# Deformable sampling: half of the odd samples' corner sums go from Pool to ACT and DVE

## Chip, core and metric

The kernel runs on one core of a Trainium2 chip. The metric is the device time of one execution in microseconds (us). PE is TensorE (matrix products and transposes into PSUM), DVE is VectorE, ACT is ScalarE, Pool is GpSimd, SP issues the DMAs.

## What is computed

The program is a network of four blocks on an input of 8 x 64 x 16 x 16; the change lies in the second block's convolution, a deformable one. Each output pixel samples its input at 9 positions that an earlier convolution has shifted, for each of 4 groups of 16 channels; a sample is the sum of 4 neighbouring pixels, each by a bilinear weight. The samples are contracted with the weights `wd`.

```python
def deform_conv(x, offset, wd, k=3, pad=1, dg=4):
    ...
    py = dy + ky[None, None, :, None, None] + hh[None, None, None, :, None]
    px = dx + kx[None, None, :, None, None] + ww[None, None, None, None, :]
    y0 = jnp.floor(py)
    x0 = jnp.floor(px)
    ...
    val = gather(y0, x0) * (wy0 * wx0)[:, :, None] + gather(y0, x0 + 1) * (wy0 * wx1)[:, :, None] + gather(y0 + 1, x0) * (wy1 * wx0)[:, :, None] + gather(y0 + 1, x0 + 1) * (wy1 * wx1)[:, :, None]
    wr = wd.reshape(wd.shape[0], dg, cg, K)
    return jnp.einsum('ogck,bgckhw->bohw', wr, val)
```

## The kernel before

Each stage of the network is a block with one hand-written instruction queue for each engine; semaphores order the engines among each other. The stage in question works on 36 samples (4 channel groups x 9 positions). The 2048 output pixels are 16 tiles of 128 partitions. For sample s:

- SP loads the sample's pixel numbers, spread over all partitions, into one of four buffers BC (512 KB a load), as soon as the masks of sample s-4 are made.
- DVE makes a 0/1 mask of the lower half of the pixels from BC (`compare`, L1279), ACT the mask of the upper half (L1202). Three buffers hold masks, so the masks of sample s wait for the gather of s-3.
- PE gathers (`gather`, L1096): 64 products of mask and pixel values into two PSUM banks, 4 to 7 in turn. It gives the 4 corners by 16 channels for each tile. It waits for both masks of s and for the weighing of s-2.
- DVE weighs the corners (`weigh`, L1289): two products of 128x512 that read PSUM and write U, of which there are two (SQ and SD). Weighing s waits for Pool's sums of s-2.
- Pool adds the four corners: a first sum of 128x512 into V1 (L1032), a wait for that, and a second of 128x256 into VAL (L1035). The last sample's sums are made by DVE (L1302, L1303).

DVE's queue in the loop is: compare(s+1), weigh(s). After eight samples PE turns their values (`contract`, L1117): 16 transposes in four groups of four. Each group fills a PSUM bank, 0 and 1 in turn, and ACT empties it into VTA (`evac`, L1195). Then PE projects them (`project`, L1130). In PE's queue the turnings stand after the gathers of samples 11, 19, 27 and 34, the projections after those of 15, 23 and 31 and at the end; a fifth turning and projection, of samples 32 to 35, follow. ACT empties the first three turnings after its masks of samples 13, 21 and 29. "First turning" and so on are these calls of `contract`; a group of eight samples is the time from one turning to the next.

Of the kernel before, what the change touches and what calls it, by code (L numbers as in the profile page):

```python
# [74 lines left out]
def build(nc, x_dram, packs, idx_dram, gate_dram, out_dram):  # L75
    with ExitStack() as ctx:
# [19 lines left out]
        def wt(name, a=0, n=None, p0=0, p1=P):  # L96
# [6 lines left out]
        w_in = [w_sems[0 if n == 0 else 2 - n % 2] for n in range(len(SECTIONS))]  # L103
        W_AT = [16 if n == 0 else 16 * ((n + 1) // 2) for n in range(len(SECTIONS))]
        stored = sem("stored")
        ln_centered, ln_squared, ln_var, ln_sd, ln_rstd, ln_spread, ln_placed, ln_copied, ln_done = (sem(n) for n in (
            "ln_centered", "ln_squared", "ln_var", "ln_sd", "ln_rstd", "ln_spread", "ln_placed", "ln_copied", "ln_done"))
        g_ps, g_exp, g_sum = (sem(n) for n in ("g_ps", "g_exp", "g_sum"))
        x_half = sem("x_half")
        EARLY = range(1, 7)  # L110
# [99 lines left out]
        def ln_dve(dve, n, out_of):  # L210
            o, view = out_of(0)
            dve.wait_ge(ln_squared, 2 * n + 1)
            dve.tensor_copy(o, view(bank(0))).then_inc(ln_placed, 1)
            for h in range(2):
                c = slice(h * STAT, (h + 1) * STAT)
                dve.wait_ge(ln_sd, 2 * n + h + 1)
                dve.reciprocal(SD[:, c], SD[:, c]).then_inc(ln_rstd, 1)
            for h in range(2):
                o, view = out_of(h)
                if h:  # L220
                    dve.wait_ge(ln_copied, n + 1)
                else:
                    dve.wait_ge(ln_placed, n + 1)
                dve.wait_ge(ln_spread, 2 * n + h + 1)
                spread = PS[:, 2048 * (1 - h):2048 * (2 - h)].rearrange("p (q c) -> p q c", q=4)[:, :, 0:P]
                if view is flat_view:
                    quarters = o.rearrange("p (q c) -> p q c", q=4)
                    ins = dve.tensor_tensor(quarters, quarters, spread, ALU.mult)  # L228
                else:
                    for b in range(2):  # L230
                        part = o[:, b].rearrange("p (k r) w -> p k r w", k=2)
                        ins = dve.tensor_tensor(part, part, spread[:, 2 * b:2 * b + 2].rearrange("p k (r w) -> p k r w", w=W), ALU.mult)
                ins.then_inc(ln_done, 1)
# [720 lines left out]
        with ExitStack() as sctx, nc.Block() as block:  # L954
# [35 lines left out]
                sem("s3_" + n) for n in ("y_pad", "c1_ps", "h_act", "h_dve", "tents_ready", "c2_ps", "gx_ps", "gx_hi", "gx_done", "idx_ready",  # L990
                "frac_ready", "idxt_ps", "idxt_in", "idx_out", "oh_ready", "ga_ps", "u_ready",
                "val_ready", "vt_ps", "vt_in", "dc_ps", "xs_ready"))
            vt_dve, wc_ready, last_val = sem("s3_vt_dve"), sem("s3_wc_ready"), sem("s3_last_val")

            bc_in = [sem(f"bc_in{i}") for i in range(NBC)]

# [27 lines left out]
            @block.gpsimd  # L1024
            def _(pool):
                pool.memset(YP[:, :, :], 0.0).then_inc(y_pad, 1)  # L1026
                for k in range(3):
                    pool.memset(HS3[k][:, :, :], 0.0).then_inc(y_pad, 1)
                for s in range(SAMPLES - 1):

                    pool.wait_ge(u_ready, s + 1)
                    after_pool(pool, pool.tensor_tensor(V1[:, :, :, :], U[s % 2][:, :, 0:2, :], U[s % 2][:, :, 2:4, :], ALU.add))  # L1032
                    if s >= 16 and s % 8 == 0:
                        pool.wait_ge(vt_ps, 4 * (s // 8 - 1))
                    pool.tensor_tensor(VAL[:, (s // 8) % 2, :, s % 8, :], V1[:, :, 0, :], V1[:, :, 1, :], ALU.add).then_inc(val_ready, 1)  # L1035
                    pool.wait_ge(val_ready, s + 1)

            @block.tensor
            def _(pe):
# [60 lines left out]
                def contract(ch):  # L1100

                    ns = min(8, SAMPLES - 8 * ch)
                    rows = ns * CG
                    pe.wait_ge(val_ready, min(8 * ch + ns, SAMPLES - 1))
                    if ch == 4:
                        pe.wait_ge(last_val, 1)
                    for j, q in enumerate(LAST if ch == 4 else range(4)):
                        n = 4 * ch + j
                        if n == 19:
                            pe.wait_ge(vt_dve, 1)  # L1110
                        elif n >= 2:
                            pe.wait_ge(vt_in, n - 1)
                        for i in range(4):

                            t = 4 * (2 * (q % 2) + i // 2) + 2 * (q // 2) + i % 2
                            src = VAL[:, ch % 2, t, 0:ns, :].rearrange("p s c -> p (s c)")
                            mm = pe.transpose(bank(j % 2)[0:rows, i * P:(i + 1) * P], src, wt("ident"))  # L1117
                        mm.then_inc(vt_ps, 1)
                    return rows

# [28 lines left out]
            @block.scalar  # L1149
            def _(act):  # L1150
                act.wait_ge(y_pad, 1)
                ln_act(act, 2, "epsc", padded_y)
                act.wait_ge(w_in[3], W_AT[3])
                act.wait_ge(y_pad, 4)
                act.wait_ge(c1_ps, 1)
                for k in range(3):

                    a, b = max(0, 1 - k), min(W, W + 1 - k)
                    act.activation(pair(HS3[k], 0, 2, 0)[:, :, :, a:b], images(bank(6))[:, :, :, a + k - 1:b + k - 1],
                                   ACT.Identity, bias=wt("c1b")).then_inc(h_act, 1)  # L1160

                def corners(n):
                    bl, qh = n // 2, n % 2
                    act.wait_ge(gx_ps, n + 1)
                    act.activation(GX[:, 0, qh, bl, :, :], bank(n % 4).rearrange("p (k c) -> p k c", k=4), ACT.Copy,
                                   scale=GSCALE).then_inc(gx_hi, 1)

                def tents(n):
                    act.wait_ge(frac_ready, n + 1)
                    for u, at in ((U0, 0.0), (U1, -1.0)):  # L1170
                        o = tiles4(u[:, :, :], n)
                        after_act(act, act.activation(o, tiles4(PY[:, :, :], n), ACT.Abs, bias=at if at == 0.0 else wt("minus1")))
                        act.activation(o, o, ACT.Relu, bias=1.0, scale=-1.0).then_inc(tents_ready, 1)

                for n in range(4):
                    corners(n)
                for n in range(3):
                    tents(n)
                for n in range(NB):
                    act.wait_ge(idxt_ps, n + 1)  # L1180
                    act.activation(tiles_of(IDXT[:, :], n), bank(4 + n).bitcast(FP16)[0:SAMPLES, 0:HC].rearrange("q (h c) -> q h c", h=2),
                                   ACT.Copy).then_inc(idxt_in, 1)
                for n in range(4, 2 * NB):
                    corners(n)

                tents(3)
                warm(act, ACT.Abs_reciprocal_sqrt)

                def evac(ch):
                    rows = P if ch < 4 else 64  # L1190
                    for j, q in enumerate(LAST if ch == 4 else range(4)):
                        if ch == 4 and j % 2:
                            continue
                        act.wait_ge(vt_ps, 4 * ch + j + 1)
                        act.activation(VTA[0:rows, ch % 4, q * 512:(q + 1) * 512], bank(j % 2)[0:rows, :], ACT.Copy,  # L1195
                                       scale=16.0 / GSCALE).then_inc(vt_in, 1)
                for s in range(SAMPLES):

                    act.wait_ge(bc_in[s % NBC], 16 * (s // NBC + 1))
                    if s >= NOH:  # L1200
                        act.wait_ge(ga_ps, s - NOH + 1)
                    act.activation(OHU[:, s % NOH, :], BC[:, s % NBC, :], ACT.Abs_reciprocal_sqrt, bias=wt("hitq"),  # L1202
                                   scale=HIT, saturate=False).then_inc(upper_ready, 1)
                    if s >= 13 and s % 8 == 5:
                        evac(s // 8 - 1)
                evac(3)
                evac(4)

                warm(act, ACT.Sqrt)

            @block.vector
            def _(dve):
# [68 lines left out]
                def weigh(s):  # L1281
# [7 lines left out]
                        ins = dve.tensor_tensor(o, src, w, ALU.mult)  # L1289
                    ins.then_inc(u_ready, 1)  # L1290

                compare(0)
                compare(1)
                dve.wait_ge(wc_ready, NB)
                for s in range(SAMPLES):
                    if 1 <= s < SAMPLES - 1:
                        compare(s + 1)
                    weigh(s)
                last = SAMPLES - 1
                sums = PY[:, :, :].rearrange("p t k -> p (t k)")[:, 0:TILES * 2 * CG].rearrange("p (t k c) -> p t k c", k=2, c=CG)  # L1300
                dve.wait_ge(u_ready, last + 1)
                after(dve, dve.tensor_tensor(sums, U[last % 2][:, :, 0:2, :], U[last % 2][:, :, 2:4, :], ALU.add))  # L1302
                dve.tensor_tensor(VAL[:, (last // 8) % 2, :, last % 8, :], sums[:, :, 0, :], sums[:, :, 1, :], ALU.add).then_inc(last_val, 1)  # L1303
                for j in (1, 3):
                    q = LAST[j]
                    dve.wait_ge(vt_ps, 16 + j + 1)
# [1101 lines left out]
```

## Time and profile before

| what | us |
|---|---|
| three runs | 539.71, 541.76, 542.22 (median 541.76) |
| the profiled execution | 541.19 |
| its span, first to last instruction | 539.4 |
| sample loop, first gather to fifth turning | 218.2 to 315.6 |
| busy in the span: PE, DVE, ACT, Pool | 478.7, 328.7, 293.0, 140.1 |

The span's whole chain passes through many stages; the change touches one. So what counts is who waits for whom between 218 and 316 us, and which engine has no idle time there. In the rows below a timeline's columns are start, duration, engine, line, operation, output and inputs, count of instructions merged in the row, and in brackets the idle time of the engine just before with what ended it. Instructions of PE follow each other in a pipeline, so a row's end lies a little after the next row's start.

### The profile page before, as it was taken

To read this page: it belongs to the slowest core of one execution; us is meant where nothing else is said; L and a number is where in the kernel's file an instruction comes from. 1 tells how busy PE (TensorE), PEld (TensorE's weight loads), DVE (VectorE), ACT (ScalarE), POOL (GpSimd) and SP (SyncE) were. 2 spreads that over 40 slices of the span, in tenths; PEclk is the share of its full clock that TensorE was granted. 3 is DMA by queue.
4 is the path that set the end of the run, shared out by engine and by line. 5 is a ranking of instruction groups with operands and counts; after the bars stand their busy time and mean duration, and the time that the engine had idled before them with its cause. 6 is when DMAs were issued, how large, how long until landed. Compare 5 with 4: busy or idle time off the path is not lost. (4 is left out here: it accounts for less than half of the span.)

```text
span 539.4 us, 12786 instructions
## 1 busy us (share of the span) xinstructions
PE 478.7 (89%) x5459; PEld 255.5 (47%) x5464; DVE 328.7 (61%) x575; ACT 293.0 (54%) x430; POOL 140.1 (26%) x134
## 2 busy tenths in 40 slices
PE   4799998998996999878998999997997998999992
PEld 1343432554333496778788744343223335533330
DVE  1285999455356366677777746758554593554565
ACT  2583223526651236988788636674683171665561
POOL 8170000000064000599999920003402000000000
PEclk9999999998998899999999998999899889999998
DMA  7000000002661002855565200011003000001000
GB/s 271 2 2 2 1 2 1 1 12 104 162 155 34 2 1 63 293 206 194 202 201 196 81 6 18 0 67 48 0 1 125 0 2 1 2 21 40 1 18 22
DMA packets 9801, 34.52 MB, mean 64 GB/s; under 512 B 1248, under 2 KB 2704, under 8 KB 9360
## 3 DMA queue, kind: packets, MB, share of 16 engines
q1 hardware_dynamic: 9744, 33.70, 19.5%
q8 instruction: 43, 0.70, 0.5%
q14 instruction: 14, 0.11, 0.1%
HBM read 32.94 MB, written 0.75 MB: 62 GB/s over the span
## 5 line engine op out<-in xcount | busy, mean ns | idle before, releaser
L1096 PE MATMUL PS<-GX,OH 128*128 128x64 f16 x1152 | 70.4, 193 | 10.0 <-DVE OH L1279 7.1
L1202 ACT ACTIVATE OHU<-BC,wbuf 128x2048 fp8e4<-128x2048 f16 x36 | 70.0, 1994 | 12.5 <-PE PS L1096 8.8
L1096 PEld LDWEIGHTS PS<-GX,OH 128*128 128x128 f16 x1152 | 67.6, 98 | 15.1 <-DVE OH L1279 8.9
L1096 PE MATMUL PS<-GX,OHU 128*128 128x64 f16 x1152 | 70.1, 193 | 0.1
L1096 PEld LDWEIGHTS PS<-GX,OHU 128*128 128x128 fp8e4 x1152 | 67.6, 98 | 0.1
L1035 POOL TENSOR_TENSOR VAL<-V 128x256 f32<-128x256 f32 x35 | 38.8, 1108 | 2.7
L708 DVE SCALAR_TENSOR_TENSOR D<-QKVP,wbuf,D 128x1024 f32<-128x1024 f32 x27 | 34.6, 1281 | 7.7 <-ACT D L608 6.9
L1032 POOL TENSOR_TENSOR V<-SQ 128x512 f32<-128x512 f32 x18 | 25.1, 1394 | 49.9 <-DVE SQ L1289 48.6
L437 PE MATMUL PS<-T,DG 128*32 128x512 f32 x336 | 37.1, 594 | 0.0
L1996 PE MATMUL PS<-Y,wbuf 64*128 64x512 f32 x128 | 35.6, 618 | 0.1
L2069 ACT ACTIVATE HID<-PS,wbuf 128x512 f32<-128x512 f32 x44 | 28.7, 689 | 10.4 <-PE PS L1996 10.3
L164 PE MATMUL PS<-X,wconst 128*128 128x512 f32 x32 | 19.6, 709 | 15.1 <-DMA wconst<-pack_dram 7.7
L1289 DVE TENSOR_TENSOR SQ<-PS,WC 128x512 f32<-128x512 f32 x36 | 23.2, 686 | 14.8 <-PE PS L1096 8.5
L824 POOL TENSOR_TENSOR ACC<-T 128x512 f32<-128x512 f32 x2 | 2.5, 1270 | 107.3 <-DVE T L938 107.3
L1279 DVE TENSOR_SCALAR OH<-BC,wbuf 128x2048 f16<-128x2048 f16 x36 | 28.1, 780 | 3.7 <-DMA BC<-idx_dram 3.7
L203 ACT ACTIVATE SQ<-PS 128x512 f32<-128x512 f32 x16 | 9.4, 595 | 38.3 <-POOL VTA L1026 11.8
L2008 PE MATMUL PS<-HID,wbuf 128*64 128x512 f32 x128 | 29.9, 601 | 0.0
L1289 DVE TENSOR_TENSOR SD<-PS,WC 128x512 f32<-128x512 f32 x36 | 23.1, 684 | 10.6 <-POOL VAL L1035 7.6
L1996 PEld LDWEIGHTS PS<-Y,wbuf 64*128 64x128 f32 x128 | 14.5, 185 | 20.3 <-issue 9.4
L608 ACT ACTIVATE D<-PS,wbuf 128x512 f32<-128x512 f32 x12 | 8.3, 689 | 28.6 <-PE PS L437 28.6
L893 ACT ACTIVATE HID<-PS,wbuf 128x512 f32<-128x512 f32 x32 | 19.4, 692 | 8.1 <-PE PS L834 8.1
L1032 POOL TENSOR_TENSOR V<-SD 128x512 f32<-128x512 f32 x17 | 22.0, 1295 | 1.3
(296 smaller groups left out, 920.3 us busy)
## 6 DMA issues: line engine op xcount, KB each, us to landing
BC<-idx_dram SPq DMA_DIRECT2D x36, 512.0 KB, 4.3
GB<-gate_dram SPq DMA_DIRECT2D x16, 256.0 KB, 7.2
wbuf<-pack_dram SPq DMA_DIRECT2D x1, 1913.0 KB, 9.3
wbuf<-pack_dram SPq DMA_DIRECT2D x1, 1624.0 KB, 6.7
wbuf<-pack_dram SPq DMA_DIRECT2D x1, 1494.0 KB, 6.1
wbuf<-pack_dram SPq DMA_DIRECT2D x1, 871.0 KB, 4.3
wbuf<-pack_dram SPq DMA_DIRECT2D x1, 788.0 KB, 10.8
wbuf<-pack_dram SPq DMA_DIRECT2D x1, 607.0 KB, 3.8
```

Of the source, the lines that this page charges most:

```text
L164: pe.matmul(bank(h), wt("center"), X[:, h * HC:(h + 1) * HC], start=True, stop=True).then_inc(ln_centered, 1)
L437: mm = pe.matmul(bank(DBANK[t % 2] + n)[32 * q:32 * q + 32, :], DG[:, (2 * j + hf) * NBLK + i, :], src, start=(i == blocks[0]), stop=(i == ...
L708: ins = dve.scalar_tensor_tensor(out=d, in0=window(QKVP[j], dy, dx), scalar=wt("dw5", j * 25 + 5 * dy + dx, 1), in1=d, op0=ALU.mult, op1=A ...
L1032: after_pool(pool, pool.tensor_tensor(V1[:, :, :, :], U[s % 2][:, :, 0:2, :], U[s % 2][:, :, 2:4, :], ALU.add))
L1035: pool.tensor_tensor(VAL[:, (s // 8) % 2, :, s % 8, :], V1[:, :, 0, :], V1[:, :, 1, :], ALU.add).then_inc(val_ready, 1)
L1096: mm = pe.matmul(o, (OH, OHU)[qh][:, s % NOH, t * P:(t + 1) * P], src, start=(qh == 0 and part == 0), stop=(qh == 1 and part == 1))
L1202: act.activation(OHU[:, s % NOH, :], BC[:, s % NBC, :], ACT.Abs_reciprocal_sqrt, bias=wt("hitq"), scale=HIT, saturate=False).then_inc(uppe ...
L1279: dve.tensor_scalar(OH[:, s % NOH, :], BC[:, s % NBC, :], wt("qidx"), 0.0625, ALU.is_equal, ALU.mult).then_inc(oh_ready, 1)
L1289: ins = dve.tensor_tensor(o, src, w, ALU.mult)
L1996: pe.matmul(bank(UBANK[(n + bh) % 4]), wt("w1_3", e * FH3 + m * P, P, r, r + C), Y[r:r + C, bp * HC:(bp + 1) * HC], start=True, stop=True, ...
L2008: pe.matmul(bank(OBANK[j % 3])[C * bh:C * bh + C, :], wt("w2_3", (2 * e + m) * C, C), HID[:, (n + i) % HBUF, :], start=(m == 0), stop=(m = ...
L2069: act.activation(HID[:, n % HBUF, :], bank(UBANK[n % 4]), ACT.Relu, bias=wt("b1_3", 2 * e + m, 1)).then_inc(hid_in_a, 1)
```

## The change

For odd samples below 32 Pool makes the first sum only, into VO (two buffers, one for each second odd sample). ACT copies one of its two halves into PSUM bank 1 (VP), after its mask of sample s+4. DVE adds the other half and VP into VAL (`corner_sum`), in its queue after the compare of s+4 and ahead of the weighing of s+3. Since bank 1 is taken, the first three turnings use bank 0 alone: each group of four transposes waits until ACT has emptied the one before. In the fourth turning the second group waits for the first's evacuation, and the two banks are used in turn. The layer norm gives up a semaphore of its own (`ln_placed`) and waits on DVE's step counter.

```diff
+            def sums_on_dve(s):
+                return s % 2 == 1 and s < 32
+            def turned(j, ch):
+                return bank(j % 2 if ch >= 3 else 0)
...
                     pool.wait_ge(u_ready, s + 1)
+                    if sums_on_dve(s):
+                        if s >= 5:
+                            pool.wait_ge(val_dve, s // 2 - 1)
+                        pool.tensor_tensor(VO[:, (s // 2) % 2, :, :, :], U[s % 2][:, :, 0:2, :], U[s % 2][:, :, 2:4, :], ALU.add).then_inc(val_ready, 1)
+                        continue
...
                     if ch == 4:
-                        pe.wait_ge(last_val, 1)
+                        pe.wait_ge(val_dve, 17)
+                    else:
+                        pe.wait_ge(val_dve, 4 * ch + 4)
...
-                        elif n >= 2:
+                        elif ch >= 3 and j >= 2 or ch == 4:
                             pe.wait_ge(vt_in, n - 1)
+                        elif n:
+                            pe.wait_ge(vt_in, n)
...
-                            mm = pe.transpose(bank(j % 2)[0:rows, i * P:(i + 1) * P], src, wt("ident"))
+                            mm = pe.transpose(turned(j, ch)[0:rows, i * P:(i + 1) * P], src, wt("ident"))
...
+                    j = s - NOH - 1
+                    if j >= 0 and sums_on_dve(j):
+                        act.wait_ge(val_ready, j + 1)
+                        if j >= 3:
+                            act.wait_ge(val_dve, j // 2)
+                        act.activation(VP, VO[:, (j // 2) % 2, :, 1, :], ACT.Copy).then_inc(vp_in, 1)
...
+                def corner_sum(s):
+                    dve.wait_ge(vp_in, s // 2 + 1)
+                    if s >= 16:
+                        dve.wait_ge(vt_ps, 4 * (s // 8 - 1))
+                    dve.tensor_tensor(VAL[:, (s // 8) % 2, :, s % 8, :], VO[:, (s // 2) % 2, :, 0, :], VP, ALU.add).then_inc(val_dve, 1)
...
                     if 1 <= s < SAMPLES - 1:
                         compare(s + 1)
+                    if s >= 3 and sums_on_dve(s - 3):
+                        corner_sum(s - 3)
                     weigh(s)
```

## Rows read from the trace of the kernel before

**Rows 1.** Busy time by stretch: stretch, length, each engine's busy time, PE clock, DMA.

```profile
236.00:246.00 10.00, 7.58 (x242) 7.11 (x239) 7.22 (x12) 7.43 (x5) 9.37 (x9) 1.00 0.58 207
```

**Rows 2.** The weighings' line (L1289), what ended DVE's idle time: us, times.

```profile
  POOL VAL L1035: 13.9, 20
```

**Rows 3.** Timeline of Pool in the loop.

```profile
237.86 1.27 POOL L1032 TENSOR_TENSOR V<-SQ 128x512 f32<-128x512 f32 x1
239.22 1.21 POOL L1035 TENSOR_TENSOR VAL<-V 128x256 f32<-128x256 f32 x1
240.51 1.28 POOL L1032 TENSOR_TENSOR V<-SD 128x512 f32<-128x512 f32 x1
```

**Rows 4.** Timeline of DVE: a weighing in the same cycle.

```profile
240.53 1.29 DVE L1289 TENSOR_TENSOR SQ<-PS,WC 128x512 f32<-128x512 f32 x2 [0.69 <-POOL VAL L1035]
```

**Rows 5.** Timeline of PE: gather 11, the first turning, gather 12.

```profile
245.18 0.23 PE L1096 MATMUL PS<-GX,OH 128*128 128x64 f16 x2 [0.60 <-DVE OH L1279]
...
247.06 1.07 PE L1117 MATMUL PS<-wconst,VAL 128*128 128x128 f32 x8
...
248.38 1.15 PE L1117 MATMUL PS<-wconst,VAL 128*128 128x128 f32 x8 [0.25 <-ACT VTA L1195]
...
249.36 0.22 PE L1096 MATMUL PS<-GX,OH 128*128 128x64 f16 x2
```

**Rows 6.** Timeline of PE: gather 14, the first projection, gather 16.

```profile
253.78 0.23 PE L1096 MATMUL PS<-GX,OH 128*128 128x64 f16 x2 [0.52 <-DVE OH L1279]
...
257.62 1.94 PE L1130 MATMUL PS<-VTA,wbuf 128*64 128x512 f32 x8
...
259.49 0.20 PE L1096 MATMUL PS<-GX,OH 128*128 128x64 f16 x1
```

**Rows 7.** Timeline of PE: starts of turnings two and three, and gather 35.

```profile
268.30 0.31 PE L1117 MATMUL PS<-wconst,VAL 128*128 128x128 f32 x1
...
289.92 0.31 PE L1117 MATMUL PS<-wconst,VAL 128*128 128x128 f32 x1
...
310.94 0.22 PE L1096 MATMUL PS<-GX,OH 128*128 128x64 f16 x2
```

**Rows 8.** Timeline of Pool: sums ahead of a compare, behind one, and alone.

```profile
252.44 0.73 POOL L1035 TENSOR_TENSOR VAL<-V 128x256 f32<-128x256 f32 x1
...
295.73 1.65 POOL L1032 TENSOR_TENSOR V<-SQ 128x512 f32<-128x512 f32 x1 [0.61 <-DVE SQ L1289]
297.45 1.25 POOL L1035 TENSOR_TENSOR VAL<-V 128x256 f32<-128x256 f32 x1
...
311.41 1.28 POOL L1032 TENSOR_TENSOR V<-SQ 128x512 f32<-128x512 f32 x1
```

**Rows 9.** Timeline of DVE at the same places as rows 8.

```profile
251.43 1.29 DVE L1289 TENSOR_TENSOR SQ<-PS,WC 128x512 f32<-128x512 f32 x2 [1.01 <-PE PS L1096]
252.64 1.08 DVE L1279 TENSOR_SCALAR OH<-BC,wbuf 128x2048 f16<-128x2048 f16 x1
...
295.50 0.74 DVE L1279 TENSOR_SCALAR OH<-BC,wbuf 128x2048 f16<-128x2048 f16 x1
296.16 1.29 DVE L1289 TENSOR_TENSOR SD<-PS,WC 128x512 f32<-128x512 f32 x2
297.36 0.75 DVE L1279 TENSOR_SCALAR OH<-BC,wbuf 128x2048 f16<-128x2048 f16 x1
```

**Rows 10.** DVE's second sum of the last sample: ns, least, median, most.

```profile
L1303 DVE TENSOR_TENSOR VAL<-PY x1: 426/426/426, 315.1 to 315.1; 128x256 f32<-128x256 f32 x1
```

**Rows 11.** A short operation of ACT, by groups: busy us, mean ns, idle before.

```profile
L206 ACT ACTIVATE SD<-PS,wconst 128x64 f32<-128x64 f32 x2 | 0.6, 311 | 0.4 <-PE PS L183 0.4
```

**Rows 12.** Timeline of ACT: an evacuation and four masks in a row.

```profile
247.73 0.60 ACT L1195 ACTIVATE VTA<-PS 128x512 f32<-128x512 f32 x1 [1.05 <-PE PS L1117]
...
271.30 7.67 ACT L1202 ACTIVATE OHU<-BC,wbuf 128x2048 fp8e4<-128x2048 f16 x4
```

**Rows 13.** Timeline of PE: inside gather 26.

```profile
287.93 0.20 PE L1096 MATMUL PS<-GX,OH 128*128 128x64 f16 x1 [1.36 <-issue]
```

More of the change, by code:

```diff
@@ L105, in build @@
         stored = sem("stored")
-        ln_centered, ln_squared, ln_var, ln_sd, ln_rstd, ln_spread, ln_placed, ln_copied, ln_done = (sem(n) for n in (
-            "ln_centered", "ln_squared", "ln_var", "ln_sd", "ln_rstd", "ln_spread", "ln_placed", "ln_copied", "ln_done"))
+        ln_centered, ln_squared, ln_var, ln_sd, ln_rstd, ln_spread, ln_copied, ln_done = (sem(n) for n in (
+            "ln_centered", "ln_squared", "ln_var", "ln_sd", "ln_rstd", "ln_spread", "ln_copied", "ln_done"))
         g_ps, g_exp, g_sum = (sem(n) for n in ("g_ps", "g_exp", "g_sum"))
@@ L212, in ln_dve @@
             dve.wait_ge(ln_squared, 2 * n + 1)
-            dve.tensor_copy(o, view(bank(0))).then_inc(ln_placed, 1)
+            steps["dve"] += 1
+            placed = steps["dve"]
+            dve.tensor_copy(o, view(bank(0))).then_inc(dve_step, 1)
             for h in range(2):
@@ L222, in ln_dve @@
                 else:
-                    dve.wait_ge(ln_placed, n + 1)
+                    dve.wait_ge(dve_step, placed)
                 dve.wait_ge(ln_spread, 2 * n + h + 1)
@@ L992, in build @@
                 "val_ready", "vt_ps", "vt_in", "dc_ps", "xs_ready"))
-            vt_dve, wc_ready, last_val = sem("s3_vt_dve"), sem("s3_wc_ready"), sem("s3_last_val")
+            vt_dve, wc_ready, val_dve, vp_in = sem("s3_vt_dve"), sem("s3_wc_ready"), sem("s3_val_dve"), sem("s3_vp_in")
+            VO = sb("VO", [P, 2, TILES, 2, CG], F32, sctx)
+            VP = bank(1, TILES * CG).rearrange("p (t c) -> p t c", c=CG)
+            def sums_on_dve(s):
+                return s % 2 == 1 and s < 32
+            def turned(j, ch):
+                return bank(j % 2 if ch >= 3 else 0)
             bc_in = [sem(f"bc_in{i}") for i in range(NBC)]
@@ L1194, in evac @@
                         act.wait_ge(vt_ps, 4 * ch + j + 1)
-                        act.activation(VTA[0:rows, ch % 4, q * 512:(q + 1) * 512], bank(j % 2)[0:rows, :], ACT.Copy,
+                        act.activation(VTA[0:rows, ch % 4, q * 512:(q + 1) * 512], turned(j, ch)[0:rows, :], ACT.Copy,
                                        scale=16.0 / GSCALE).then_inc(vt_in, 1)
@@ L1302, in _ @@
                 after(dve, dve.tensor_tensor(sums, U[last % 2][:, :, 0:2, :], U[last % 2][:, :, 2:4, :], ALU.add))
-                dve.tensor_tensor(VAL[:, (last // 8) % 2, :, last % 8, :], sums[:, :, 0, :], sums[:, :, 1, :], ALU.add).then_inc(last_val, 1)
+                dve.tensor_tensor(VAL[:, (last // 8) % 2, :, last % 8, :], sums[:, :, 0, :], sums[:, :, 1, :], ALU.add).then_inc(val_dve, 1)
                 for j in (1, 3):
```

## Prediction

> Everything below is worked against the profiled execution of the kernel before: 541.19 us, of which 539.4 are its span and 1.8 lie around it. The median of the runs shown is 541.76, so a difference found here would stand 0.6 higher against that. G(s), W(s), C(s) stand for sample s's gather on PE, weighing on DVE (L1289) and compare on DVE (L1279).
>
> **What bounds the kernel now.** I read the busy time by stretch first, then who waited for whom, then the timelines. In the sample loop Pool is the busiest engine, 9.37 of 10 us, with PE at 7.58 and its clock at 1.00 [rows 1]. Weighing waited 20 times for Pool's second sum [rows 2]. The timelines give the cycle: Pool's first sum starts at 237.86 and again at 240.51, so a sample costs 2.65 us: 1.28 for the first sum, 1.21 for the second, two gaps of 0.08 [rows 3]; the next weighing starts 0.1 after the second sum ends and had waited 0.69 [rows 4]. But a group of eight samples also holds a turning (16 transposes) and a projection, and there PE has hardly any slack. A gather has 1.88 us from its start to the next work (245.18 to 247.06), the first turning 2.30 (to 249.36) [rows 5], a projection 1.87 [rows 6]. 8 x 1.87 + 2.30 + 1.87 = 19.1 us of PE work, and the groups take 268.30 - 247.06 = 21.24 and 289.92 - 268.30 = 21.62 [rows 5, 7]. So Pool's relief can win at most some 2.3 us a group before PE is the bound.
>
> **Pool, odd samples below 32.** The second sum leaves Pool. Its price there is 0.73 when nothing disturbs it [rows 8] and 1.21 here, because DVE's compare and Pool's sums shut each other out: a sum that begins 0.1 behind a compare takes 1.25 in place of 0.73, or 1.65 in place of 1.28; a compare that begins 0.2 behind a sum took 1.08 and ended 0.55 after it [rows 8, 9]. For two samples Pool then holds two first sums (2 x 1.28), one second (0.73), three gaps (0.25) and still two compares that push in (0.5 each): 4.5 us, 2.25 a sample in place of 2.65. Pool stays the bound until the first turning: DVE needs 2 x (1.21 + 0.66) + 0.35 = 4.1 a pair (1.21 and 0.66 are the distances between the starts of its operations, 0.35 that of the corner sum, each 0.08 less than it lasts), and G(s+2) follows G(s) by at least 2.07 to W, 1.21 to C, 0.74 for C and 0.06 to PE = 4.08 [rows 5, 6, 9]. Samples 4 to 11 run so; the first of them is still paced by loads and PE, so I take 7.3 of them x 0.40 = **2.9 us gained by the first turning** (bounds: 2.0 and 4.3, by 4.75 and by 4.1 us a pair).
>
> **The two new operations.** DVE adds 16 corner sums of 128x256. The same shape took 0.43 [rows 10]; that its second operand lies in PSUM I cost at nothing, since two 128x512 weighings, which read PSUM too, take 1.29, and Pool's first sum beside them keeps its 1.28 [rows 3, 4, 8]. 16 x 0.43 = 6.9 us, all beside PE and Pool except one (below). The sum stands before W(s), so weighing and every compare behind it queue on ACT's copy. For odd j that copy stands behind ACT's mask of j+4, which starts when G(j+1) ends; the corner sum stands behind C(j+4), which follows W(j+2), and so comes about 1 us after the copy. ACT adds 16 copies of 128x256 to PSUM, which no row shows: between 0.31 (128x64) and 0.60 (128x512), by proportion 0.43 [rows 11, 12]. A pair on ACT is 2 x 1.9 + 0.4 = 4.2, under 4.5. Behind them wait ACT's masks and its evacuations. In a group ACT is just in time: from the end of G(16) it has three masks and two copies, 3 x 1.9 + 2 x 0.35 = 6.4, and the next turning's first values are ready after 6.4. With copies of 0.60 it is 0.5 late, twice.
>
> **One bank for the turned values.** This is the costly part. Before, PE turned two groups of four back to back and waited only 0.25 for the third [rows 5]. Now, in the first three turnings, each group waits until ACT has emptied the bank: first transpose to evacuation 0.67 (247.06 to 247.73), evacuation 0.60, back to PE 0.06: 1.32 a round [rows 5, 12]. Three rounds and the last group's issue, 3 x 1.33 + 0.49 = **4.5 in place of 2.3: 2.2 us each**. In the fourth, only its second group waits for the first's evacuation and the last for the second's: 2 x 1.32 + 0.49 = 3.1, 0.8 more.
>
> **The groups after.** PE: 4.5 + 8 x 1.87 + 1.87 + two waits of 0.34 (the 4.08 above against 2 x 1.87, once behind the turning, once behind the projection; between them DVE catches up) = **22.0 us**. Pool's 4 x 4.5 = 18.0 no longer matters: the bound has moved to PE. Against 21.24 and 21.62 that is +0.75 and +0.4. The last stretch, from the third turning to G(35) (310.94 - 289.92 = 21.0 before [rows 7]), has seven gathers: 4.5 + 7 x 1.87 + 1.87 + 0.7 = 20.1, then the fourth turning waits 0.35 for the last corner sum, which DVE reaches only behind C(35) (a compare delayed, or not, sets this: 0 to 0.8), and takes 3.1: 23.6, +2.6. After G(35) nothing is changed.
>
> **A stall that was covered.** In the second of these groups PE stood 1.36 us inside a gather, put down to issue [rows 13]. Pool was the bound there, so part of it was covered: that group took 21.62 against 21.24. In the new kernel PE is the bound and the same stall counts whole, on top of the 22.0. It may not come back (0) or come as it was (1.36); the instructions around it are the same, so I take the row, 1.36. The Trainium skill's page "Runtime: NRT & Kernel Launch", section "Instruction fetch mechanics", says that fetching code across a block boundary is mostly hidden; if this is such a fetch and hidden the next time, the sum below is smaller by 1.36. The row shows only that it was not hidden here.
>
> Costed at nothing: the layer norm's own semaphore given up for DVE's step counter (the same wait on the same copy); PE's extra wait on the corner sums before the first three turnings (the sum of the group's last odd sample is done 1.5 us earlier, by the order on DVE); Pool's wait for a free half of VO (two odd samples back). No DMA is added; the loads of BC are asked for by the same masks.
>
> **Sum:** 541.19 - 2.9 + 0.75 + 0.4 + 2.6 = 542.0, and with the stall 543.4; from the unrounded terms **543.3 us**.
>
> **The rivals.**
> (a) The stall does not return: **542.0**. For it: one gather of 36 shows it. Against: the same code at the same place.
> (b) Slower, the compare loses to Pool's second sum. In an even-odd pair C(s+3) is ready 0.08 before Pool could start the second sum of s. The trace shows it winning by 0.09 (297.36 against 297.45) and the sum then taking 1.25 [rows 8, 9]. If it comes 0.1 later it waits out 0.73 and ends 0.62 later: G(15) and G(19) of every group are late by that, 2 x 0.62 x 3 = 3.7, and the first stretch gains 2.0 only: 543.3 + 3.7 + 0.9 = **547.9**. It decides from a shift of 0.1 us, such as a longer corner sum makes. The Trainium skill's page "SBUF — State Buffer", section "Who interferes with whom", has it as an exclusive lock that whoever issues first holds for a whole instruction; the rows above agree (0.55 after the sum's end). Whoever drops this sentence keeps the rows.
> (c) ACT is late: copies at 0.60 bring 2 x 0.5, and evacuations a little: **544.5**.
> (d) Faster, the rounds of the one bank stay off the path: a group would be 19.1 + 0.7 = 19.8, and the stage would win 2.9 + 1.4 + 1.8 + 0.9 = 7: **534**. Against: the waits are in PE's own queue ahead of the next gather, and PE has 2.1 us to spare a group where they cost 2.2. For: should weighing and compares now run far enough ahead, some of PE's other waits go too.
> (e) The copy is not what delays, but the change does not relieve Pool (a compare hits all three sums): 5 us a pair, and the first stretch gains 1: **545**.
>
> **How the numbers follow.** Forecast with stall 0.36, (a) 0.24, (b) 0.13, (c) 0.10, (d) 0.10, (e) 0.07. The range runs from 540.0 ((a) with the first stretch at its better bound) to 547.0 (the unknown copy and most of (b)). About 0.5%, 2.7 us, is what a measurement of this kernel can tell from no change. From 541.19 that puts (a) and seven tenths of the forecast's own scatter inside, with a fifth of (c); (b), (e), the rest of (c) and of the forecast above, less what the better bound of the first stretch takes back; (d) below: same 0.52, slower 0.37, faster 0.11.
>
> **What would show it.** First turning at 244 us in place of 247; distances between turnings of 22 to 23.4; three PE waits for ACT of some 0.8 in each of the first three turnings; Pool idle between an odd sample's sum and the next; PE waiting for DVE's masks by 0.3 and not 0.6. It is wrong if turnings stay near 2.3, if the groups fall under 21 us, or if compares of 1.1 and more become common.

## The result: 0.85% slower, and the profile after

Twenty runs of the changed kernel have a median of 545.38 us (540.51 to 552.67), twenty of the kernel before 539.65 (535.89 to 542.83). The ratio is 1.0085, with a 95% interval of 1.0054 to 1.0115, or some 4.6 us; it leaves out runs over 1.5% above the kernel's fastest, six of the changed kernel's twenty, so it is below the 5.7 us between the medians. The profiled execution took 544.75 us, its span 542.9. Forecast were 543.3 (540.0 to 547.0): the time lies in the range, but the loss is a bit more than twice the 2.1 us forecast, and the outcome that was given most weight, no change within 0.5%, is not the one that came.

Stretch by stretch the costs that the forecast names came close to their sizes. Pool's timeline in the first stretch, two samples:

```profile
236.48 1.71 POOL L1049 TENSOR_TENSOR V<-SQ 128x512 f32<-128x512 f32 x1
238.27 1.25 POOL L1052 TENSOR_TENSOR VAL<-V 128x256 f32<-128x256 f32 x1
239.59 1.28 POOL L1047 TENSOR_TENSOR VO<-SD 128x512 f32<-128x512 f32 x1
240.99 1.71 POOL L1049 TENSOR_TENSOR V<-SQ 128x512 f32<-128x512 f32 x1
```

The pair lasts 240.99 - 236.48 = 4.51 us, two samples before 5.29 [rows 3]. Both sums of the even sample stand behind a compare here, at 1.71 and 1.25; not all do (see rival (b) below). The two new operations, by line (ns: least, median, most), DVE's corner sum and ACT's copy:

```profile
L1323 DVE TENSOR_TENSOR VAL<-VO,PS x16: 406/411/417, 230.2 to 312.7; 128x256 f32<-128x256 f32 x16
```

```profile
L1230 ACT ACTIVATE PS<-VO x16: 363/367/376, 229.3 to 310.9; 128x256 f32<-128x256 f32 x16
```

Both are a little cheaper than 0.43 [rows 10 to 12]. PE's timeline of the first turning shows the rounds through one bank:

```profile
246.00 0.31 PE L1138 MATMUL PS<-wconst,VAL 128*128 128x128 f32 x1
...
247.32 0.33 PE L1138 MATMUL PS<-wconst,VAL 128*128 128x128 f32 x1 [0.69 <-ACT VTA L1216]
...
248.66 0.33 PE L1138 MATMUL PS<-wconst,VAL 128*128 128x128 f32 x1 [0.69 <-ACT VTA L1216]
...
250.01 0.33 PE L1138 MATMUL PS<-wconst,VAL 128*128 128x128 f32 x1 [0.69 <-ACT VTA L1216]
...
250.50 0.19 PE L1113 MATMUL PS<-GX,OH 128*128 128x64 f16 x1
```

PE waits 0.69 for ACT three times, and 250.50 - 246.00 = 4.50 us pass where 2.30 did [rows 5]. Behind it the bound has changed. What ended DVE's idle time before the weighings (us, times), in the kernel before:

```profile
  PE PS L1096: 11.5, 10
```

and in the kernel after:

```profile
  PE PS L1113: 23.3, 12
  POOL VAL L1052: 2.6, 7
```

Weighing waits for PE where it waited 13.9 us for Pool [rows 2]. Two stretches behind the first turning, with the columns of rows 1 (behind the length come the busy times of PE, PE's weight loads, DVE, ACT and Pool), before:

```profile
256.00:266.00 10.00, 9.43 (x258) 7.76 (x254) 7.64 (x12) 7.99 (x5) 9.37 (x9) 1.00 0.63 214
276.00:286.00 10.00, 9.82 (x277) 8.27 (x274) 7.21 (x12) 8.30 (x5) 9.45 (x8) 1.00 0.66 214
```

and after:

```profile
256.00:266.00 10.00, 9.82 (x278) 8.27 (x274) 8.49 (x15) 8.95 (x7) 8.67 (x7) 1.00 0.65 224
296.00:306.00 10.00, 9.23 (x266) 8.48 (x268) 6.48 (x11) 9.25 (x9) 5.87 (x5) 1.00 0.44 153
```

Pool is down from 9.37 and 9.45 to 8.67 and 5.87. PE's busy time alone doesn't show the change: it was 9.43 and 9.82 here already, and 7.58 only in the stretch of rows 1, which holds no turning. The stretches' lengths, read from PE's timeline (us; T1 is the first turning, G35 the last gather):

| stretch | before | forecast | after | after, minus before |
|---|---|---|---|---|
| first gather to T1 | 28.90 | 26.0 | 26.89 | -2.0 |
| T1 to T2 | 21.24 | 22.0 | 22.11 | +0.9 |
| T2 to T3 | 21.62 | 23.4 | 24.47 | +2.9 |
| T3 to G35 | 21.02 | 23.6 | 23.76 | +2.7 |
| loop | 92.78 | 95.0 | 97.23 | +4.5 |

Of the 2.2 us that the forecast lacked, 0.9 is in the first line (a late load and a stall, see below) and 1.1 in the third. There a stall of 0.64 stood where 1.36 was forecast, and the clock shows the rest. Stretches around the end of the second turning (the last number but two is PE's granted clock):

```profile
270.00:272.00 2.00, 0.74 (x5) 0.42 (x4) 1.01 (x3) 1.13 (x2) 1.89 (x2) 1.00 0.66 229
272.00:273.00 1.00, 0.88 (x4) 0.85 (x5) 0.00 (x0) 0.06 (x1) 0.61 (x1) 0.55 0.93 352
273.00:274.00 1.00, 1.00 (x20) 0.97 (x18) 0.00 (x0) 0.73 (x2) 0.00 (x0) 0.50 0.55 205
274.00:275.00 1.00, 1.00 (x23) 1.00 (x21) 0.00 (x0) 1.00 (x1) 0.00 (x0) 0.50 0.10 41
276.00:277.00 1.00, 1.00 (x41) 1.00 (x38) 0.78 (x2) 0.71 (x1) 0.00 (x0) 1.00 0.09 16
```

PE is granted 0.50, 1.2 GHz, and makes 23 products a microsecond where it makes 41 at 1.00. Before that it had been busy 0.74 of 2 us, in the rounds of the turning.

### The profile page after: what moved, and what is told of

Same layout as the page of the kernel before. It is cut to its first block and busy times, and to the rows that moved or that the text cites. A ratio compares the mean times of both kernels' runs of the same rounds, so it can differ in the third digit from the quotient of the medians.

```text
span 542.9 us, 12810 instructions
## 1 busy us (share of the span) xinstructions
PE 478.1 (88%) x5459; PEld 257.7 (47%) x5464; DVE 332.0 (61%) x591; ACT 297.9 (55%) x446; POOL 128.4 (24%) x118
## 5 line engine op out<-in xcount | busy, mean ns | idle before, releaser
L1049 POOL TENSOR_TENSOR V<-SQ 128x512 f32<-128x512 f32 x18 | 30.3, 1686 | 66.3 <-DVE SQ L1316 65.6
L2031 PE MATMUL PS<-Y,wbuf 64*128 64x512 f32 x128 | 36.8, 645 | 0.1
L2179 DVE COPY_PREDICATED SUM<-MINE,OUT 128x512 f32<-128x512 uint16 x14 | 10.3, 735 | 18.9 <-ACT OUT L2097 18.8
L1047 POOL TENSOR_TENSOR VO<-SD 128x512 f32<-128x512 f32 x16 | 21.4, 1336 | 1.5 <-DVE SD L1316 0.3
```

What stands on the lines that cost most here:

```text
L1047: pool.tensor_tensor(VO[:, (s // 2) % 2, :, :, :], U[s % 2][:, :, 0:2, :], U[s % 2][:, :, 2:4, :], ALU.add).then_inc(val_ready, 1)
L2031: pe.matmul(bank(UBANK[(n + bh) % 4]), wt("w1_3", e * FH3 + m * P, P, r, r + C), Y[r:r + C, bp * HC:(bp + 1) * HC], start=True, stop=True, ...
```

## The experiments

Theory A: the loss comes from PE's rounds through one bank. Rival B: it comes from the longer chain from Pool over ACT to DVE. Later C to F were about what the forecast lacked. Ratios are to the kernel before, with the 95% interval.

**Sums from SBUF, two banks.** ACT's copy is gone, DVE adds both halves of VO, the turned values alternate between the banks.

```diff
-                return bank(j % 2 if ch >= 3 else 0)
+                return bank(j % 2)
...
-                        elif ch >= 3 and j >= 2 or ch == 4:
+                        elif n >= 2:
                             pe.wait_ge(vt_in, n - 1)
-                        elif n:
-                            pe.wait_ge(vt_in, n)
...
-                        act.activation(VP, VO[:, (j // 2) % 2, :, 1, :], ACT.Copy).then_inc(vp_in, 1)
...
-                    dve.wait_ge(vp_in, s // 2 + 1)
+                    dve.wait_ge(val_ready, s + 1)
...
-                    dve.tensor_tensor(VAL[:, (s // 8) % 2, :, s % 8, :], VO[:, (s // 2) % 2, :, 0, :], VP, ALU.add).then_inc(val_dve, 1)
+                    dve.tensor_tensor(VAL[:, (s // 8) % 2, :, s % 8, :], VO[:, (s // 2) % 2, :, 0, :], VO[:, (s // 2) % 2, :, 1, :], ALU.add).then_inc(val_dve, 1)
```

> The changed kernel without ACT's copy: DVE adds both halves of VO straight from SBUF, and the turned values use two banks again. Theory A (PE's rounds through one bank are what the change loses): turnings last 2.3 us again, the first one starts about 2 us earlier than in the kernel before, groups of eight take 19.8 to 20.5 us, and the whole is 3 to 5 us faster than the kernel before. Theory B (the longer chain from Pool to DVE and the two new waits are what it loses): it stays 2 us or more slower than before. On the side: if the corner sum with two SBUF inputs shuts Pool out, a pair of samples costs 4.9 us before the first turning, otherwise 4.5.

Measured: 539.68 us, ratio 0.9994 (0.9957 to 1.0030). In the profile the turnings are back at 2.31 and the groups at 19.92 and 20.69, the loop at 89.21, 3.6 under that of the kernel before: theory A holds in the loop, but the time is only level with it, between A's and B's. The corner sum's line:

```profile
L1315 DVE TENSOR_TENSOR VAL<-VO x16: 954/960/1481, 228.5 to 303.5; 128x256 f32<-128x256 f32 x16
```

0.96 us where it took 0.41 with one operand in PSUM. The sum of [rows 10] has both operands in SBUF too and took 0.43, with Pool done; so what delays it is Pool's sum beside it. One of each:

```profile
233.07 1.25 POOL L1052 TENSOR_TENSOR VAL<-V 128x256 f32<-128x256 f32 x1
```

```profile
233.64 0.96 DVE L1315 TENSOR_TENSOR VAL<-VO 128x256 f32<-128x256 f32 x1
```

The corner sum begins inside Pool's second sum and ends 0.28 after it. The pairs take 4.60, nearer the 4.5 than the 4.9 expected on the side: the price falls on DVE more than on Pool. DVE is busy 10.00 of 10 us in the first stretch:

```profile
230.00:240.00 10.00, 8.08 (x271) 7.84 (x268) 10.00 (x16) 8.40 (x5) 8.26 (x6) 1.00 0.61 223
```

**The same once more.**

> The sums from SBUF with two banks once more, since its sample loop was 3.6 us shorter in the profile while its times were level with the kernel before. If the profile is right: 2 to 4 us faster than the kernel before. If not: level again, and then stalls or half-speed stretches in other executions eat what the loop wins.

540.26 us, ratio 1.0020 (0.9983 to 1.0056): level again, while the profiled loop took 90.06. Its runs lie between 534.0 and 545.8. The two profiled executions took 537.35 and 538.52, 2.3 and 1.7 below their medians, so they are among the faster ones; where the others lose what the loop wins in these was not found.

**One bank alone**, in the kernel before.

```diff
-                        elif n >= 2:
+                        elif ch >= 3 and j >= 2 or ch == 4:
                             pe.wait_ge(vt_in, n - 1)
+                        elif n:
+                            pe.wait_ge(vt_in, n)
...
-                            mm = pe.transpose(bank(j % 2)[0:rows, i * P:(i + 1) * P], src, wt("ident"))
+                            mm = pe.transpose(bank(j % 2 if ch >= 3 else 0)[0:rows, i * P:(i + 1) * P], src, wt("ident"))
...
-                        act.activation(VTA[0:rows, ch % 4, q * 512:(q + 1) * 512], bank(j % 2)[0:rows, :], ACT.Copy,
+                        act.activation(VTA[0:rows, ch % 4, q * 512:(q + 1) * 512], bank(j % 2 if ch >= 3 else 0)[0:rows, :], ACT.Copy,
                                        scale=16.0 / GSCALE).then_inc(vt_in, 1)
```

> The kernel before with one bank for the first three turnings and nothing else. Theory A: each of the first three turnings takes 4.5 us, the fourth 3.1. Pool stays the bound but now stands idle about 1.7 us behind each, so groups take 22.9 us and the whole is 5 to 6.5 us slower than before; Pool's relief then won 1 to 2 us of that back in the changed kernel. Theory B: the rounds are covered by PE's 2.1 us of slack a group, and the whole is at most 1.5 us slower.

548.48 us, ratio 1.0150 (1.0108 to 1.0192), 8.1 us: more than A expected, and B's at most 1.5 is out. Pool's timeline behind the first turning:

```profile
252.98 0.73 POOL L1035 TENSOR_TENSOR VAL<-V 128x256 f32<-128x256 f32 x1
257.17 1.65 POOL L1032 TENSOR_TENSOR V<-SQ 128x512 f32<-128x512 f32 x1 [3.47 <-DVE SQ L1291]
```

Pool stands idle 3.47, not 1.7. With it goes a gather at half speed:

```profile
252.00:253.00 1.00, 1.00 (x17) 0.94 (x16) 0.00 (x0) 0.48 (x1) 0.92 (x2) 0.50 0.65 262
253.00:254.00 1.00, 1.00 (x23) 1.00 (x21) 0.00 (x0) 1.00 (x2) 0.71 (x1) 0.50 0.68 250
```

The second turning had the same, for longer; the third had none, and took the 4.50 us of A. The one bank thus costs by itself more than the whole change loses, and Pool's relief gives some of it back.

**The turnings cut up**, in the changed kernel: one group of four transposes behind each of four gathers, the one bank and all the rest kept.

```diff
...
-                    if s in (11, 19, 27, 34):
-                        contract(s // 8 - 1)
+                    if 11 <= s < 31 and s % 8 in (3, 4, 5, 6):
+                        contract(s // 8 - 1, [s % 8 - 3])
+                    if s == 34:
+                        contract(3)
...
-                    if s >= 13 and s % 8 == 5:
-                        evac(s // 8 - 1)
+                    if 13 <= s < 33 and (s - 5) % 8 < 4:
+                        evac((s - 13) // 8, [(s - 5) % 8])
...
```

What is left out lets `contract` and `evac` take one group of the four.

> The changed kernel, but each of the first three turnings is cut up: one group of four transposes after each of four gathers, so that ACT empties the one bank while PE gathers. Theory A: PE hardly waits for ACT any more, groups take 19.8 to 20.3 us, the stretch from the third turning to gather 35 some 21.4, and the whole is 3 to 5 us faster than the kernel before. Theory B: groups stay at 21.5 us or more, and the whole is as slow as the changed kernel.

536.57 us, ratio 0.9936 (0.9908 to 0.9964): 3.5 us faster than the kernel before, some 8 faster than the changed one. The turnings' starts:

```profile
246.59 0.31 PE L1143 MATMUL PS<-wconst,VAL 128*128 128x128 f32 x1
```

```profile
266.58 0.31 PE L1143 MATMUL PS<-wconst,VAL 128*128 128x128 f32 x1
```

```profile
286.31 0.31 PE L1143 MATMUL PS<-wconst,VAL 128*128 128x128 f32 x1
```

Groups of 19.99 and 19.73 us; the last stretch took 22.7, with 1.6 us of stalls in it, where 21.4 was expected. Pool, ACT's copy and DVE's corner sum do all that they do in the changed kernel. So B is out: only the places of the transposes, with PE's waits, and of ACT's evacuations were changed.

**Cut up, two banks, sums from SBUF.** The two edits above together.

> DVE adds both halves from SBUF, two banks, and the turnings cut up over four gathers. Theory A: PE waits for nobody in the turnings, groups take 19.5 to 20 us, and the whole is 3 to 5 us faster than the kernel before, as with the cut turnings and one bank. If the cutting itself is of no use, it is as the run with sums from SBUF alone.

537.06 us, ratio 0.9968 (0.9939 to 0.9997); groups of 19.73 and 20.73 and the shortest loop, 88.12. Both cut kernels beat both kernels of this case, this one just clear of level; which of the two is better the intervals don't tell.

**The changed kernel again.**

> The changed kernel again, for PE's stalls put down to issue. If they belong to the code, they stand at the same instructions as in its first profile (0.6 us in gather 9, 0.5 in the second turning, 1.1 in gather 20 or 21, 0.6 in gather 26); if they come from what else happens at that time, they stand elsewhere or are gone, and the groups without one take 22.0 us. The time should be 3 to 6 us over the kernel before either way.

544.27 us, ratio 1.0101 (1.0059 to 1.0144). No half-speed stretch in its loop, and groups of 22.12 and 22.11. Its stalls were in gathers 3 and 5 (0.93 and 1.13), so they don't belong to one instruction. Pool and DVE behind the second of them show one thing more:

```profile
238.45 0.74 POOL L1052 TENSOR_TENSOR VAL<-V 128x256 f32<-128x256 f32 x1
...
241.34 1.71 POOL L1049 TENSOR_TENSOR V<-SQ 128x512 f32<-128x512 f32 x1 [0.47 <-DVE SQ L1316]
...
246.02 1.71 POOL L1049 TENSOR_TENSOR V<-SQ 128x512 f32<-128x512 f32 x1 [0.47 <-DVE SQ L1316]
```

```profile
238.60 1.13 DVE L1306 TENSOR_SCALAR OH<-BC,wbuf 128x2048 f16<-128x2048 f16 x1
```

The compare comes 0.15 behind Pool's second sum, the sum takes 0.74 and not 1.25, the compare 1.13 and not 0.74, Pool then stands idle 0.47, and a pair takes 4.68 (246.02 - 241.34) and not 4.51. This is the order of rival (b).

**PE kept busy in the rounds**, in the changed kernel.

```diff
...
                         mm.then_inc(vt_ps, 1)
+                        if ch < 3 and j < 3:
+                            for _ in range(5):
+                                pe.matmul(bank(2)[0:C, 0:256], ZW[:, 0:C // 2].bitcast(BF16), wconst[:, AT["ident"][1]:AT["ident"][1] + 128].bitcast(BF16), start=(ch == 0), stop=(ch == 0))
...
```

What is left out makes the zeros ZW and waits for them before the loop.

> The changed kernel, and in each of the first three turnings PE multiplies five times by zeros while it waits for ACT (0.6 of the 0.7 us that it waits; the zeros go to a projection bank, where they change nothing). The rounds stay as long. Theory C (PE's idle rounds let its clock fall to 0.50 behind a turning, as at 272 us in the changed kernel's profile, and that is the part of the loss that the forecast lacked): no stretch of the sample loop is below 1.00, groups take 22.0 to 22.3 us apart from stalls put down to issue, and the whole is 1.5 to 3 us slower than the kernel before. Theory D (the stalls are that part): the whole stays 4 to 5 us slower.

545.14 us, ratio 1.0135 (1.0099 to 1.0172). What the profile should show is there, 1.00 behind each turning, here the second:

```profile
271.00:274.00 3.00, 2.98 (x56) 2.53 (x57) 0.04 (x1) 1.63 (x3) 0.84 (x1) 1.00 0.48 186
274.00:277.00 3.00, 2.82 (x98) 2.70 (x95) 2.17 (x4) 3.00 (x2) 0.80 (x1) 1.00 0.03 7
```

But the time is no better: the interval is 5.3 to 9.3 us slower than the kernel before, over C's 1.5 to 3 and just over D's 4 to 5. The profiled loop took 96.99, in stretches of 25.92, 22.88, 22.11 and 26.09; those over the shortest seen (22.11 and 23.75) are the two that hold its stalls, 0.59 and 1.98. So C is not confirmed as the missing part, and D fits better.

**The kernel before again.**

> The kernel before once more, for what its time and its sample loop do by themselves: groups of 21.2 us, 1.00 as PE's clock in the whole loop, the ratio within 0.4% of 1, and the stall put down to issue at another gather than 26 or gone.

541.08 us, ratio 1.0028 (0.9989 to 1.0067), 1.00 in the whole loop, groups of 21.94 and 21.45. The stall was not one but five:

```profile
PE PS L1096 <- issue: 5.5, 5, 1.4
```

5.5 us of PE's waits, and yet the loop took only 93.60.

**Four more executions**, two of each kernel.

> One more execution of the changed kernel, for the share of PE's stalls and half-speed stretches. Theory E: first gather to gather 35 takes 93.9 us (25.9 + 22.1 + 22.1 + 23.8) and on top of that, whole, every stall put down to issue inside a gather (0.4 to 1.5 us each, two or three in a loop) and about 1.6 us for a half-speed stretch behind a turning. Rival F: stalls are covered here too, and the loop takes 94 to 95 us whatever they are.

> As the run before it, the same kernel: 93.9 us and the stalls on top by theory E, 94 to 95 us by rival F.

> One more execution of the kernel before. Theory E: Pool covers PE's stalls, so the loop takes 92.5 to 94 us whatever they are, as in the run with 5.7 us of them. Rival F: it grows with them as the changed kernel's.

> As the run before it, the same kernel: 92.5 to 94 us by theory E.

All profiled executions of the two kernels, loop from the first gather to G35 and stalls of over 0.25 us put down to issue within gathers:

| | loop | stalls | half speed behind turnings |
|---|---|---|---|
| before | 92.78 | 1.4 | 0 |
| before, again | 93.60 | 5.5 | 0 |
| before, two more | 94.12, 91.89 | 2.6, 0.5 | 0, 0 |
| after | 97.23 | 1.2 | 1 |
| after, again | 96.14 | 2.1 | 0 |
| after, two more | 102.66, 93.91 | 3.7, 0.0 | 3, 0 |

The execution at 93.91 is the changed kernel with nothing on top. The starts of its first three turnings and of G35, from 216.89 on:

```profile
242.81 0.31 PE L1138 MATMUL PS<-wconst,VAL 128*128 128x128 f32 x1
```

```profile
264.93 0.30 PE L1138 MATMUL PS<-wconst,VAL 128*128 128x128 f32 x1
```

```profile
287.04 0.31 PE L1138 MATMUL PS<-wconst,VAL 128*128 128x128 f32 x1
```

```profile
310.79 0.19 PE L1113 MATMUL PS<-GX,OH 128*128 128x64 f16 x1
```

25.92, 22.12, 22.11 and 23.75: theory E's 93.9. With 2.1 us of stalls it takes 2.2 more; with 3.7 and three half-speed stretches, in an execution of 551.09 us, 8.8 more. Behind its three turnings, where that execution has no stall, the stretches are 2.2, 1.5 and 1.6 longer, so about 1.7 for a half-speed stretch. The first profile of the changed kernel agrees: T2 to T3 takes 2.36 more than 22.11, 0.64 of it a stall. So for the changed kernel E holds and F doesn't.

For the kernel before E doesn't hold as it stands: what a stall costs depends on its place. One execution has 5.0 us more of stalls than the one at 91.89 and takes 1.7 more. The other (94.12) has 2.1 more, takes 2.2 more and lies above E's bound. Its stalls of 0.53 and 1.71 came behind the third turning:

```profile
288.43 0.31 PE L1117 MATMUL PS<-wconst,VAL 128*128 128x128 f32 x1
```

```profile
298.61 0.19 PE L1096 MATMUL PS<-GX,OHU 128*128 128x64 f16 x1 [1.71 <-issue]
```

```profile
311.34 0.19 PE L1096 MATMUL PS<-GX,OH 128*128 128x64 f16 x1
```

From there to G35 it took 22.9, against 20.7 in the execution at 91.89, so nothing was covered. Ahead of the first turning most was: from the start of G(4) to T1 the kernel before took 20.38 in three executions and 21.00 with 2.95 us of stalls. The changed kernel took 17.28 there with none, 19.16 with 1.13 and 20.19 with 3.17. Why the last stretch of the kernel before covers nothing was not tested.

The time outside the loop varied from 445.3 to 450.4 us over the fourteen profiled executions of all kernels here, so a single execution's time tells less than its loop.

## Why the prediction was right in kind and short in size

- **The bound** was read rightly: 4.51 us a pair where 4.5 was given, PE at 22.1 us a group where 22.0 was given, and Pool idle behind it. Two readings were loose. The 9.37 and 7.58 of [rows 1] hold for a stretch without a turning and not for the whole loop, though the sum of 19.1 us a group puts that right; and the first sum of 1.65 began 0.23 behind its compare, not 0.1 [rows 8, 9], on which nothing hangs.
- **First stretch:** 25.92 us undisturbed, 3.0 gained, forecast 2.9. The first profile after shows 2.0: there G(1) started 0.34 later behind G(0) than in the kernel before, since a load of BC came late, and PE stalled 0.58.
- **One bank:** 4.50 and 3.15 us, forecast 4.5 and 3.1. It is the cause of the loss: put into the kernel before by itself, it costs 8.1 us; its waits taken out by cutting the turnings up, the kernel is 3.5 us faster than before instead of 4.6 slower.
- **The two operations** cost 0.41 and 0.37, and ACT was in time: its first evacuation stood ready 0.43 ahead in the first turning.
- **The stall** is a term that was mis-sized. I took the one of 1.36 as belonging to its place. It belongs to many places: the fourteen profiles show 34 stalls of over 0.25 us, all at products of PE that are, to within one, multiples of 127 apart (254 instructions with the weight loads), none to five of them in a loop, 0.3 to 1.7 us each. In the changed kernel's four loops they come to 1.2, 2.1, 3.7 and 0.0 us, so 1.36 was near their mean by luck. That they count whole once PE is the bound held: 0.59 cost 0.77 and 1.98 cost 2.33 behind turnings of the filled kernel. What the prediction did not have is that they count ahead of the first turning too, where it kept Pool as the bound: 1.13 cost 1.9 there (19.16 against 17.28).
- **PE's clock** is the term that was missing: it was put at nothing. I took 1.00 from rows with idle times of 0.6 a gather [rows 1, 5] and drew no conclusion for the rounds, in which PE works 0.74 of 2 us. Half speed followed 6 of 15 such turnings in the five profiles that have them without filling, and none of the 18 with two banks or the 6 cut ones. It costs about 1.7 us where it comes. That the three filled turnings had none proves little: at 6 in 15, three without would come by chance about once in five. How much of the 4.6 us this is over many executions stays open: the filled kernel's times did not fall.
- Of the rivals, (b) came in part. In undisturbed stretches compares stay ahead and the second sum takes 1.25. Ahead of the first turning, where a stall or a late load had pushed the gathers back, 3 of 5, 4 of 5 and 5 of 5 second sums took 0.73 to 0.75 in three of the changed kernel's profiles; in the two without a stall there (the one at 93.91 and the filled kernel's) none did. So it adds to what a stall costs, at 4.68 a pair in place of 4.51, and is not the lasting order that (b) priced at 3.7 + 0.9: behind the turnings most second sums took 1.25 in every profile of the changed kernel. (a), the stall gone, is the execution of 539.21 us, 93.91 in the loop; that it lies below (a)'s 542.0 comes from the rest of the program, 3.1 us shorter than in the profile worked from. (c), (d) and (e) are out by the 0.37, the 22.1 and the 4.51.
- The undisturbed sum was 92.78 + 0.8 = 93.6 against 93.91 measured. It is close in part by luck, since the 92.78 holds the 1.36 stall, which made its group some 0.5 longer than the shortest (21.62 against 21.10). From the least disturbed loop before, 91.89, the change loses 2.0. The means of the four loops each are 93.1 and 97.5, a loss of 4.4; so by this estimate, from few executions, about half of the loss is the change by itself and half is stalls and half speed that the kernel before covers or doesn't have. The chance of slower was too low: what a bound engine's slack absorbs is lost along with the slack, and that should have been counted for all of PE's irregularities, not for one.

## What to carry to other kernels

When work leaves the bounding engine, sum up the next engine's work in the same period before counting a gain; here it had 2.1 us to spare a group, and the change took 2.2 of it for the bank that it needed. If a buffer must be single, put other work of the producer between its uses: with four transposes behind each of four gathers a group took 19.7 to 20.0 us, with sixteen in a row 22.1. And an engine that has just become the bound shows every stall that the old bound hid, so look for these in more than one profile.

## What the runs showed of the hardware

- PE was granted half its clock (0.50, 1.2 GHz) behind 6 of 15 turnings of four short bursts with 0.69 us of idleness between them, and behind none of the 24 with two banks or cut up. With products by zeros in the gaps it stayed at 1.00 in the three turnings seen.
- PE's stalls inside gathers come where code is loaded: in the trace's DMA records each of the 34 ends 1.2 to 1.6 us after a record of 16384 bytes on queue 8, the one that the page of the profile calls "instruction", has ended. Where PE passed such a place without a stall, the record had ended at least 1.2 us before as well. Samples, read from the records (us):

```
kernel           record ends   PE goes on   PE idle
before           286.54        287.93       1.36
after            289.21        290.59       0.64
before, again    267.03        268.30       1.22
before, again    277.95        279.42       1.37
```

  The Trainium skill's page "Runtime: NRT & Kernel Launch", section "Instruction fetch mechanics", tells of 16 KiB blocks of 256 instructions, which fits the size and the distance, and says the cost is mostly hidden. Here a loop of some 18 blocks shows none to five that are not.
- A corner sum on DVE with both operands in SBUF took 0.96 us beside Pool, with one in PSUM 0.41. The page "SBUF — State Buffer" of the Trainium skill, section "Who interferes with whom", has two SBUF inputs against a GpSimd reader as an exclusive lock; the runs agree (0.43 alone, 0.96 begun inside Pool's sum), and the copy into PSUM for 0.37 us of ACT is a way around it.
